# Two mixture-of-experts loops over slot tiles: later stages for each tile, other buffer counts, four weight offsets per register load

## What is computed

```python
scores = jax.nn.softmax(xf @ gate_w.T, axis=-1)
weights, indices = jax.lax.top_k(scores, TOPK)
...
def body(y, inp):
    w1e, w2e, w3e, we = inp
    h = jax.nn.silu(xf @ w1e.T) * (xf @ w3e.T)
    return (y + h @ w2e.T * we[:, None], None)
...
z = jax.nn.silu(xf @ sw1.T) * (xf @ sw3.T) @ sw2.T
return (y + z).reshape(shape)
```

## Time and profile before

| | us |
|---|---|
| median of 3 runs | 1512.65 (1505.83 to 1520.51) |
| span of the profiled execution | 1507.6 |
| TensorE busy | 1343.1 (89%) |
| VectorE, ScalarE, GpSimd busy | 895.4, 789.8, 443.7 |
| mixture 0, slot tiles | about 453 to 569 |
| mixture 1, slot tiles | about 1267 to 1489 |

### The profile page before, as it was taken

The page is one execution under the profiler, slowest core; times in us unless marked ns, Lnnn a source line. Parts: engine busy times, 40 slices in busy tenths (PEclk is TensorE's granted clock), DMA queues, the critical chain, the costliest instruction groups (busy, mean ns, idle before and its releaser), DMA issues.

```text
span 1507.6 us, 22930 instructions
## 1 busy us (share of the span) xinstructions
PE 1343.1 (89%) x6461; PEld 909.5 (60%) x6461; DVE 895.4 (59%) x2649; ACT 789.8 (52%) x1907; POOL 443.7 (29%) x577
## 2 busy tenths in 40 slices
PE   6699899878799996999999999999999788999994
PEld 5334343335566665777777777777777555555552
DVE  5678687744645564655666667666767554333554
ACT  3367566544315444666656566655676332444442
POOL 6345444211446443000000150014101514444442
PEclk9689898987889998999999999999999979999997
DMA  7643534005115432243000010001000193334553
GB/s 234 149 91 88 125 104 70 2 1 227 53 64 158 132 105 91 71 143 124 1 1 15 1 51 7 15 1 43 15 15 2 58 402 103 114 112 141 167 141 117
DMA packets 79208, 134.01 MB, mean 89 GB/s; under 512 B 13788, under 2 KB 52708, under 8 KB 77420
## 3 DMA queue, kind: packets, MB, share of 16 engines
q1 hardware_dynamic: 62128, 92.39, 19.6%
q0 software_dynamic: 15712, 38.25, 9.0%
q10 hardware_dynamic: 1248, 1.90, 0.4%
HBM read 77.20 MB, written 60.00 MB: 91 GB/s over the span
## 4 chain that ended last, share of the span: by engine, by line
PE 70%; DVE 11%; issue 6%; DMA 6%; ACT 4%; POOL 3%; SPq 0%; DVEq 0%; ACTq 0%; POOLq 0%
PE psum L2622 9%; PE psum L126 9%; PE psum L1984 8%; PE psum L128 8%; PE psum L127 8%; PE psum L2501 4%; PE psum L1955 4%; PE psum L2668 3%; PE psum L854 3%; PE psum L883 3%; PE psum L2649 2%; PE psum L2535 2%; PE psum L2597 2%; PE psum L778 1%; POOL slots L1635 1%
## 5 line engine op out<-in xcount | busy, mean ns | idle before, releaser
L790 DVE TENSOR_REDUCE a_nmax<-psum 128x2 f32<-128x1024 f32 x128 | 155.1, 1217 | 65.2 <-PE psum L778 64.1
L2691 POOL DMA_INDIRECT results<-r_fin,r_to x134 | 135.4, 1011 | 192.0 <-ACT r_fin L2683 182.5
L869 ACT ACTIVATE a_et<-psum 128x512 f32<-128x512 f32 x256 | 139.0, 594 | 87.7 <-PE psum L854 84.1
L1930 ACT ACTIVATE a_spare<-psum,a_nmax 128x128 f32<-128x128 f32 (+3 forms) x256 | 134.9, 527 | 89.5 <-DVE a_nmax L1919 86.1
L1919 DVE CUSTOM_DVE_ANT_0 psum<-psum,a_spare 128x128 f32<-128x128 f32 (+3 forms) x256 | 126.8, 495 | 82.2 <-PE psum L128 81.2
L1984 PE MATMUL psum<-a_et,a_v 128*128 128x512 f32 (+3 forms) x512 | 170.8, 436 | 0.0
L2622 PE MATMUL psum<-m_w,m_xT 128*128 x536 | 163.6, 428 | 2.9 <-ACT m_xT L2605 1.7
L1964 ACT ACTIVATE a_et<-psum 128x128 f32<-128x128 f32 (+3 forms) x256 | 111.7, 436 | 67.3 <-PE psum L1955 63.9
L126 PE MATMUL psum<-a_kT,a_q 128*128 128x128 f32 (+3 forms) x256 | 119.6, 467 | 6.7 <-DVE a_q L1858 5.9
L854 PE MATMUL psum<-a_stk 50*128 50x512 f32 x256 | 107.8, 487 | 14.9 <-ACT a_et L869 12.4
L1955 PE MATMUL psum<-ident,a_spare 128*128 128x128 f32 x640 | 113.7, 275 | 1.1 <-DVE a_spare L1943 1.1
(11 more groups left out here) (326 smaller groups left out, 2983.9 us busy)
## 6 DMA issues: line engine op xcount, KB each, us to landing
r_xs<-slots SPq DMA_DIRECT2D x134, 129.0 KB, 2.2
slots<-empty SPq DMA_DIRECT2D x12, 1290.0 KB, 6.1
m_w<-in_experts SPq DMA_DIRECT2D x16, 768.0 KB, 15.1
stacks<-a_qk SPq DMA_DIRECT2D x32, 256.0 KB, 3.8
a_stk<-stacks POOLq DMA_DIRECT2D x32, 256.0 KB, 6.8
r_shared_hid<-results SPq DMA_DIRECT2D x12, 512.0 KB, 4.0
m_w<-in_experts SPq DMA_DIRECT2D x4, 1216.0 KB, 14.5
a_stk<-stacks POOLq DMA_DIRECT2D x32, 128.0 KB, 6.6
```

The lines of the kernel that those rows point to most:

```text
L790: dve.tensor_reduce(nmax[:, G % 2, qt, 2 * p:2 * p + 2], psum[:, n:n + 2, :], AX.X, ALU.max, negate=True).then_inc(s_max.sem, 1)
L869: act.activation(et[:, n % NET, 2 * p + hh, :], psum[:, 4 + hh, :], ACT.Exp).then_inc(s_e.sem, 1)
L1930: act.activation(e[:, u % NE, 0:W], psum[:, n, 0:W], ACT.Exp, bias=nmax[:, u % NE, :], scale=-1.0, accum_out=rsum[:, u % NE, :]).then_inc( ...
L2691: pool.indirect_dma_start(results[:, :], bass.IndirectOffsetOnAxis(ap=to[:, i % NI, 0:1].bitcast(U32), axis=0), ys[:, o, :], None, bounds_ ...
```

## The change

A tile's up product moves from one step behind its rows to two, its hidden turn and down product from two to four, its scaling and scatter from two to five. In a step TensorE now turns the new rows first. ScalarE scales first, then copies the rows, then does silu. `xT` and `hd` get three buffers, `silu` and `hdT` keep two. The register load takes four tiles' offsets in one instruction, without the check of its range on the chip, in the step ahead of the first of them. The steps of the sums and of the next norm move back by three, and the loop has three steps more.

```diff
@@ -2347,10 +2347,10 @@
         sb = lambda name, shape, dt=F32: k.sb(outer, f"m{l}_" + name, shape, dt)
         norm = Norm(k, outer, f"m{l}", l, 1, 0, B, n_xn=TT, h32=normed)
         w = sb("w", [P, WS + n_exp * WE])
-        NT3 = 2
+        NT3, NT2, STARTS = 3, 2, 4
         xT = sb("xT", [P, NT3, KT, P])
-        silu, hd = sb("silu", [P, NT3, hid]), sb("hid", [P, NT3, hid])
-        hdT = sb("hidT", [CH, NT3, NC, P])
+        silu, hd = sb("silu", [P, NT2, hid]), sb("hid", [P, NT3, hid])
+        hdT = sb("hidT", [CH, NT2, NC, P])
         w_at = sb("w_at", [1, P], I32)
         s_wsh, s_wex, s_kept = k.sem("dma_w_shared"), k.sem("dma_w_experts"), [k.sem(f"dma_kept{b}") for b in range(B)]
@@ -2606,14 +2606,20 @@
                                ACT.Copy).then_inc(s_xTc.sem, 1)
                 banks.free[xsT_bank[i]] = xTc_done[i] = s_xTc.up()
-            def tensor_start(i):
-
+            def tensor_starts(i):
+
+                if i == 0:
+                    pe.wait_ge(*at["w_at"])
+                last = min(i + STARTS, n_tiles)
+                loads, starts = k.nc.values_load_multi_w_load_instructions(
+                    w_at[0:1, i:last], engines=[mybir.EngineType.PE], min_val=WS, max_val=WS + (n_exp - 1) * WE,
+                    skip_runtime_bounds_check_because="the table holds WS + WE * expert, with 0 <= expert < n_exp")
+                for n in range(last - i):
+                    start_of[i + n] = starts[n]
+
+            def tensor_up(i):
                 if i == 0:
                     pe.wait_ge(*experts_in)
-                    pe.wait_ge(*at["w_at"])
-                start_of[i] = pe.value_load(w_at[0:1, i:i + 1], min_val=WS, max_val=WS + (n_exp - 1) * WE)
-
-            def tensor_up(i):
                 up_bank[i] = n = up_banks.next()
                 if up_banks.free[n]:
                     pe.wait_ge(*up_banks.free[n])
...
@@ -2665,12 +2671,12 @@
                     pe.wait_ge(*y_banks.free[n])
                 pe.wait_ge(*hTc_done[i])
                 for c in range(NC):
-                    mm = pe.matmul(psum[:, n, 0:D], hdT[:, i % NT3, c, :],
+                    mm = pe.matmul(psum[:, n, 0:D], hdT[:, i % NT2, c, :],
                                    w[0:CH, bass.ds(start_of[i] + KT * 2 * hid + c * D, D)], start=(c == 0),
                                    stop=(c == NC - 1))
                 mm.then_inc(s_down.sem, 1)
                 down_done[i] = s_down.up()
-                pe.free_register(start_of[i].val)
+                pe.free_register(start_of[i].val.handles[0])
             def scalar_ys(i):
                 if i >= NY:
@@ -2696,7 +2702,7 @@
-            NEXT_STAT, NEXT_SD, NEXT_ROWS = (22, 23, 24, 25, 30, 31, 32, 33), 33, (35, 36)
+            NEXT_STAT, NEXT_SD, NEXT_ROWS = (25, 26, 27, 28, 33, 34, 35, 36), 36, (38, 39)
             nn, next_bank = next_norm, {}
             def tensor_next_rows(half):
@@ -2741,7 +2747,7 @@
             LAST_TILE = [min((b + 1) * TT * picked + E - 2, n_tiles - 1) for b in range(B)]
             EVERY = picked - 1
-            SUM_AT = {SL + LAST_TILE[b] + 4 + EVERY * t: b * TT + t for b in range(B - 1) for t in range(TT)}
+            SUM_AT = {SL + LAST_TILE[b] + 7 + EVERY * t: b * TT + t for b in range(B - 1) for t in range(TT)}
             wide = s_hid_b[:, :, :, :].rearrange("p a c s -> p (a c s)")
             room_of = [wide[:, i * picked * D:(i + 1) * picked * D] for i in range(2 * NSC * S // (picked * D))]
             combine = Combine(k, l, picked, gate_rows, room_of)
@@ -2786,23 +2792,21 @@
                 if s == SL - 3 and wmod is not None:
                     tensor_next_modulation()
                 i = s - SL
-                if i == 0:
-                    tensor_start(0)
-                if 0 <= i - 2 < n_tiles:
-                    tensor_hidT(i - 2)
-                if 0 <= i - 1 < n_tiles:
-                    tensor_up(i - 1)
-                if 0 < i < n_tiles:
-                    tensor_start(i)
                 if next_norm and i in NEXT_ROWS:
                     tensor_next_rows(NEXT_ROWS.index(i))
                 if 0 <= i < n_tiles:
                     tensor_xsT(i)
+                if 0 <= i - 4 < n_tiles:
+                    tensor_hidT(i - 4)
+                if 0 <= i - 2 < n_tiles:
+                    tensor_up(i - 2)
+                if 0 <= i - 1 < n_tiles and (i - 1) % STARTS == 0:
+                    tensor_starts(i - 1)
             def tensor_late(s):
-                if 0 <= s - SL - 2 < n_tiles:
-                    tensor_down(s - SL - 2)
+                if 0 <= s - SL - 4 < n_tiles:
+                    tensor_down(s - SL - 4)
             def vector(s):
                 if s == 0 and not done:
@@ -2852,8 +2856,8 @@
                 i = s - SL
                 if 0 <= i < n_tiles:
                     vector_to(i)
-                if 0 <= i - 2 < n_tiles:
-                    vector_hidT(i - 2)
+                if 0 <= i - 4 < n_tiles:
+                    vector_hidT(i - 4)
                 for j in range(picked):
                     if s - 2 - j in SUM_AT:
                         combine.vector_step(SUM_AT[s - 2 - j], j)
@@ -2866,8 +2870,8 @@
                     for c in range(NSC):
                         if UP_AT[b][c] == s:
                             vector_shared_hid(b, c)
-                if 0 <= s - SL - 1 < n_tiles:
-                    vector_hid(s - SL - 1)
+                if 0 <= s - SL - 2 < n_tiles:
+                    vector_hid(s - SL - 2)
             def scalar(s):
                 for b in todo:
@@ -2891,12 +2895,12 @@
                         scalar_natural(b, 0)
                         scalar_natural(b, 1)
                 i = s - SL
-                if 0 <= i - 1 < n_tiles:
-                    scalar_silu(i - 1)
+                if 0 <= i - 5 < n_tiles:
+                    scalar_ys(i - 5)
                 if 0 <= i < n_tiles:
                     scalar_xT(i)
                 if 0 <= i - 2 < n_tiles:
-                    scalar_ys(i - 2)
+                    scalar_silu(i - 2)
                 if weights1 and 0 <= i - 1 < weights1.n_early:
                     weights1.scalar_hi(i - 1)
                 if next_norm:
@@ -2917,8 +2921,8 @@
                         if DOWN_AT[b][pair] == s and not done:
                             gpsimd_fin(b, pair)
                 i = s - SL
-                if 0 <= i - 2 < n_tiles:
-                    gpsimd_out(i - 2)
+                if 0 <= i - 5 < n_tiles:
+                    gpsimd_out(i - 5)
                 if weights1 and 0 <= i - 1 < weights1.n_early:
                     weights1.gpsimd_lo(i - 1)
                 if next_norm and i in NEXT_ROWS:
@@ -2941,7 +2945,7 @@
                 norm.vector_rstd()
             for t in range(TT):
                 norm.vector_xn(done, t, t)
-            for s in range(SL + n_tiles + 3):
+            for s in range(SL + n_tiles + 6):
                 sync(s)
                 tensor(s)
                 vector(s)
```

More of the change, by code:

```diff
@@ L2628, in scalar_silu @@
             def scalar_silu(i):
-                if i >= NT3:
-                    act.wait_ge(*hid_done[i - NT3])
+                if i >= NT2:
+                    act.wait_ge(*hid_done[i - NT2])
                 act.wait_ge(*up_done[i])
-                act.activation(silu[:, i % NT3, :], psum[:, up_bank[i], 0:hid], ACT.Silu).then_inc(s_silu.sem, 1)
+                act.activation(silu[:, i % NT2, :], psum[:, up_bank[i], 0:hid], ACT.Silu).then_inc(s_silu.sem, 1)
                 silu_done[i] = s_silu.up()
@@ L2638, in vector_hid @@
                 dve.wait_ge(*silu_done[i])
-                dve.tensor_tensor(hd[:, i % NT3, :], silu[:, i % NT3, :], psum[:, up_bank[i], hid:2 * hid],
+                dve.tensor_tensor(hd[:, i % NT3, :], silu[:, i % NT2, :], psum[:, up_bank[i], hid:2 * hid],
                                   ALU.mult).then_inc(s_hid.sem, 1)
@@ L2654, in vector_hidT @@
             def vector_hidT(i):
-                if i >= NT3:
-                    dve.wait_ge(*down_done[i - NT3])
+                if i >= NT2:
+                    dve.wait_ge(*down_done[i - NT2])
                 dve.wait_ge(*hT_done[i])
-                dve.tensor_copy(hdT[:, i % NT3].rearrange("p c s -> p (c s)"),
+                dve.tensor_copy(hdT[:, i % NT2].rearrange("p c s -> p (c s)"),
                                 psum[0:CH, hT_bank[i], 0:NC * P]).then_inc(s_hTc.sem, 1)
```

## The result

| | before | changed |
|---|---|---|
| median, us | 1514.18 (1505.83 to 1520.51) | 1448.27 (1442.99 to 1457.88) |
| span of the profiled execution | 1507.6 | 1448.8 |
| mixture 0, first rows' turn to last down | 114.4 | 106.5 |
| mixture 1, the same | 221.0 | 165.1 |
| step of mixture 1 / 0, median from up to up | 2.26 / 2.67 | 1.67 / 2.49 |

The ratio is 0.959, with a 95% interval of 0.955 to 0.963; 1450 had been predicted. The same kernel measured twice more (e7 and e12, on two chips) gave 0.959 [0.955, 0.964] and 0.963 [0.956, 0.970].

What follows compares the result with a forecast made beforehand. TensorE's waits were taken to bound it: 2.26 us a tile in mixture 1 against a 1.63 floor. Span 1507.6 less 52.7 (mixture 1) and 10 (mixture 0) is 1445, plus 5.05 to the median: 1450 us, range 1432 to 1478.

Steps and rivals of the forecast that it cites:

- The hole and the late start: TensorE idle 0.4 us before the hidden turn, up then 0.1 us slower; both go, 0.5 us per tile.
- The offsets' load: Register load behind up on TensorE's sequencer delays the rows' turn; its 0.13 us per tile in mixture 1 goes.
- The load of four: Loading four offsets costs as one, 0.31 us, hidden behind up; upper bound 1.24 us, +12 us in mixture 1.
- Down's wait: Down waits for the copy of its own step's hidden turn; 0.07 us a tile left for it.
- Sum tiles: In mixture 1, 36 tiles with sums take 1.82 us, the other 59 take 1.70; VectorE's costliest step is 2.0.
- Tight, but met: A sum's load lands in 4.0 us and is used about 2.7 steps, 4.6 us, after it starts.
- Filling and emptying: Three steps more to empty and one to fill the loop: 2.5 us in mixture 1.
- Mixture 0, -10: Mixture 0 falls from 114.4 to 103.8 us, counted as -10; first 12 tiles 2.83 us each, other 27 2.53.
- GpSimd's pace: Rival: the 0.84 us before a scatter doesn't overlap the one ahead; tile 1.87 us, total 1462 us; chance 0.11.
- VectorE's pace: Second rival: list copy waits up to 0.98 us for scatters; tiles 1.75, 2.3 with sums; total 1471 us; chance 0.10.
- TensorE's sequencer: Rival: register arithmetic, waits or a long load of four stay in the way; tile 1.95 us, 1470 us; chance 0.09.
- The fifth rival: Slower: ScalarE's scaling waits for the scatter four tiles before to land; at 10 us landing 1555 us; chance 0.01.

Runs made afterwards that it cites:

- e7: The changed kernel measured again without an edit; 1449.4 us, ratio 0.959 to the kernel before.
- e12: The changed kernel measured a third time without an edit, on a fourth chip; 1456.3 us, ratio 0.963 to the kernel before.
- e9: Changed kernel with hidden turn and down three steps behind the rows instead of four, up still two; 1507.5 us, ratio 0.997 to the kernel before.
- e5: Changed kernel with two buffers of xT and hd instead of three; 1450.9 us, ratio 0.963 to the kernel before.
- e2: Kernel before with four offsets per load and no range check, its order, distances and buffers kept; 1516.9 us, ratio 1.001.
- e3: Changed kernel with one offset per load instead of four, without the range check; 1458.2 us, ratio 0.962 to the kernel before.
- e4: Changed kernel with the hidden turn ahead of the rows' turn in each step; 1460.9 us, ratio 0.965 to the kernel before.
- e8: Changed kernel with up one step behind its rows, hidden turn and down three, scaling and scatter four; 1440.6 us, ratio 0.955.
- e1: Changed kernel with the offset load of before, one per tile with its range check; 1457.4 us, ratio 0.963 to the kernel before.
- e10: Changed kernel with e8's distances, a third room for sums, additions three steps behind their load, six result buffers; 1449.1 us, ratio 0.957.

## Why the prediction was right, and where it was not

*The hole and the late start go by the distance, 0.5 us a tile*: right, and too little. Without the distance all 0.59 us are gone (e9); 0.04 of them need the third buffers as well (e5). The hole itself was read too large: down's second pass started at 1313.52, not 1313.44, so that a third could have started at 1313.73, 0.33 us ahead of the turn and not 0.4.

*The offsets' load, 0.13 us a tile*: wrong. The hole and the load are not added up: they lie beside each other, and the chain through ScalarE and VectorE was the longer. The step that failed was to split 0.63 us of idle time by its places on TensorE instead of asking what closes the cycle: the earlier trace rows had it, 2.03 us from up to turn and 0.23 from turn to up. The prediction was not hurt, as hole and load went together; that is luck, for with the load gone alone it would have been 10 us and more too low (e2).

*The load of four, lower bound taken*: right. It takes 0.33 us in the median against 0.30 for one in the same order (e3). In the old order it takes 0.50 against 0.31 (e2 and before), so it isn't free everywhere. The Trainium skill's 200 ns per register ("Runtime: NRT & Kernel Launch", Instruction fetch mechanics), which that page gives for registers loaded from HBM, doesn't hold here, where the table lies in SBUF: three more values cost 0.03 to 0.19 us, not 0.6. The estimate of 1457 us from it was also too high by its own terms: with the cover of the upper bound, 1.24 - 0.5 = 0.74 us, a load of 0.91 us would be 0.17 us too long, not 0.3.

*Down's wait, 0.07 us a tile above 1.63*: right in kind, 0.04 in size (e4).

*Sum tiles 1.82, 36 of them, from VectorE's costliest step*: the amount too high by half or more (36 x 0.15 = 5.4 us above 1.67, measured 2.4 to 3.4), the mechanism wrong. VectorE takes the costliest step from its reserve; what costs are loads that land late, in five or six places. "Tight, but met" was the step that failed: the use was counted from the load's place in the program, not from the moment at which its room comes free.

*Filling and emptying, 2.5 us*: 165.1 - 95 x 1.667 - 2.8 leaves 3.9; the 2.8 are all steps above 1.667 us less those below it.

*Mixture 0, -10*: -7.9. The first 12 tiles were not held to 2.83 us by the weights' loads, which now came 2.63 us apart (468.61 to 487.05): they took 31.3 us, not 34, of which two steps took 4.19 and 3.13 and the others mostly 2.5. At the start silu of the second tile stands on ScalarE behind a copy that waits 1.54 us for the weights; it is a step later in the loop than before. VectorE does that tile's product and its list copy (0.60 us) before it copies the first hidden turn, and down(0) waits 1.44 us:

```profile
463.48 0.63 ACT L1689 ACTIVATE a_wkv_hi<-a_stage 128x512 fp32r<-128x512 f32 x1 [1.54 <-DMA a_stage<-in_w_kv]
...
465.39 0.41 DVE L2664 COPY m_hidT<-psum 88x256 f32<-88x256 f32 x1
466.05 1.12 PE L2674 MATMUL psum<-m_w,m_hidT 88*128 x4 [1.44 <-DVE m_hidT L2664]
```

e8, in which silu stands ahead of that copy, has 2.54 and 2.49 there, and mixture 0 is 1.7 us shorter. At the end TensorE no longer waits for the product behind the table load, and the granted clock stays at 1.00 there (545 to 553 us; 0.79 before). But two steps, 3.50 and 3.44 us, hold the next norm's turns and 0.34 and 0.51 us of waiting ahead of them, and the emptying has waits of its own, with its last down at the lower level of 1.2 GHz (granted clock 0.50 from 564 to 567 us):

```profile
562.00 1.12 PE L2674 MATMUL psum<-m_w,m_hidT 88*128 x4 [1.28 <-DVE m_hidT L2664]
...
564.12 2.07 PE L2674 MATMUL psum<-m_w,m_hidT 88*128 x4 [0.77 <-DVE m_hidT L2664]
```

*The rivals.* GpSimd's pace: no; a scatter comes every 1.67 us, as TensorE's step does, and where two queue they are still 1.29 us apart. VectorE's pace: no; the list copy takes less than before, 16.4 us in mixture 1 for 25.9. TensorE's sequencer: no; with a load in every step the steps are 1.67 us too (e1, e3). The fifth rival's wait exists, 0.7 us in two places, far from its price.

The total came out within 2 us partly by luck, since misses cancel. Mixture 1 gave 3.2 us more than predicted, mixture 0 2.1 less, and attention 0 took 5.8 in this profile: span 1448.8 in place of 1445. And the 5.05 us by which the median lay above the span was no constant: it now lies 0.5 below.

## What to carry to other kernels

Where an engine's order holds a tile's next product one step behind the last, write down the cycle that closes through the other engines, and compare it with the engine's own work: the longer one is the step, and nothing taken from the shorter one counts. One more step of distance, within the new order, was worth 0.59 us a tile, and a second where no chain needed it (rows to up) gave nothing and cost 1.7 us in mixture 0. A transfer's time must be counted from what lets it start (the buffer that comes free), and when steps get shorter, so do all such reserves: at 1.67 us a step a load of 4 to 6 us was late two steps ahead of its use, and no longer with three steps and a free room (e10).

## What the runs showed of the hardware

Loading four offsets from SBUF into registers takes TensorE's sequencer 0.33 us in the median, loading one 0.30 (24 and 95 times in mixture 1, changed kernel and e3). In the old order it is 0.50 (e2) against 0.31 (before), so the time depends on what stands around the load, too.

VectorE's copy of two columns became shorter as scatters on GpSimd came closer together, in the mean 0.273 us before and 0.175 after (95 copies each), where the prediction feared the opposite. The two do not meet less often: 90 copies start while a scatter runs before, 85 after. What differs is where in the scatter the copy starts (a scatter lasts 0.98 us by the profile, whose times on GpSimd are rough). After the change 69 of the 95 start 0.4 to 0.5 us behind a scatter's start, and take 0.16 us like those that meet none; before, 21 start 0.5 to 0.6 us behind it, and take 0.39 us in the mean. With two buffers (e5) 74 start 0.6 to 0.7 us behind it and take 0.32. So the scatter did not hold the copy for its whole length, as the second rival assumed, and its share of the time says little about the copy's.

After a gap between products up's four passes take 1.12 to 1.13 us (before, e9), without one 1.03 (changed, e4), at a granted clock of 1.00 in both.
